# The first norms of a two-branch transformer block become steps of the expert units' schedule

## The reference, cut to what matters

```python
xn = layernorm(x)                      # the first norm: (x - mean) / sqrt(var + eps)
out = x + encoder(xn) + experts(xn)

def experts(x):                        # one attention of 8 heads, no mask
    xn = layernorm(x, norm_w, norm_b)
    q, k, v = project(xn)              # token quarter e reads only the first 128 / 2**e features
    a = softmax(q @ k.T * 128 ** -0.5) @ v
    return out_project(a) + x          # again cut to 128 / 2**e features

def encoder(x):                        # 4 layers, 16 heads, causal with ALiBi
    for i in range(4):
        x = x + mha(layernorm(x, ln1_w[i], ln1_b[i]))
        x = x + ffn(layernorm(x, ln2_w[i], ln2_b[i]))      # gelu, 512 hidden
    return layernorm(x, final_w, final_b)
```

## Time and profile before

| | |
|---|---|
| median of three runs | 1554.06 us |
| the profiled execution, its own time | 1555.07 us |
| its span, first to last instruction | 1553.0 us |
| TensorE busy | 1424.0 us (92%) |
| ScalarE busy | 1232.2 us (79%) |
| VectorE busy | 1069.0 us (69%) |
| GpSimd busy | 633.2 us (41%) |
| mean granted TensorE clock | 0.973 |

### The profile page before, as it was taken

One profiled execution on the slowest core, in us unless ns is written; L12 is line 12 of the kernel. 1 busy time (PEld: TensorE's weight loads), 2 busy tenths in 40 slices (PEclk: granted clock), 3 DMA queues, 4 the chain that ended last, 5 costly groups with the idle time before them and its releaser, 6 DMA issues.

```text
span 1553.0 us, 39617 instructions
## 1 busy us (share of the span) xinstructions
PE 1424.0 (92%) x10720; PEld 934.6 (60%) x10720; DVE 1069.0 (69%) x2802; ACT 1232.2 (79%) x2181; POOL 633.2 (41%) x1087
## 2 busy tenths in 40 slices
PE   2779997599999999999999999999999999999995
PEld 2455554256666666666666666666666666666653
DVE  5677774366777777777777767777777777777762
ACT  3334454178899999999999989999999999999884
POOL 4444444333333333333333333333333345555443
PEclk9989997689999999999999999999999999999998
DMA  6324441244444454544444445444444455444430
GB/s 181 103 83 123 122 122 62 82 122 115 128 123 128 123 127 124 143 134 128 123 122 123 129 128 136 129 128 130 122 123 131 135 142 135 133 130 129 127 93 11
DMA packets 106534, 187.78 MB, mean 121 GB/s; under 512 B 20104, under 2 KB 72456, under 8 KB 106448
## 3 DMA queue, kind: packets, MB, share of 16 engines
q1 hardware_dynamic: 91632, 150.45, 34.9%
q0 software_dynamic: 14848, 36.72, 9.0%
HBM read 120.87 MB, written 65.01 MB: 120 GB/s over the span
## 4 chain that ended last, share of the span: by engine, by line
PE 65%; DVE 13%; issue 9%; DMA 5%; ACT 3%; POOL 3%; SPq 1%; DVEq 0%; POOLq 0%; ACTq 0%
PE pvp L1141 13%; DVE negm L815 10%; PE mxp L1084 10%; PE exp_ps L1118 9%; PE dense L1182 6%; PE mxp L1030 6%; PE mxp L1088 6%; PE dense L1059 4%; PE dense L1170 3%; DMA blocks<-split_L 3%; PE mxp L1069 2%; PE dense L1030 2%; PE mxp L1159 2%; PE mxp L1059 1%; DMA split_F<-lo 1%
## 5 line engine op out<-in xcount | busy, mean ns | idle before, releaser
L815 DVE TENSOR_REDUCE negm<-mxp 128x2 f32<-128x512 f32 x896 | 568.1, 685 | 58.1 <-PE mxp L1088 55.1
L974 ACT ACTIVATE probs<-exp_ps 128x512 f32<-128x512 f32 x896 | 514.5, 593 | 105.9 <-PE exp_ps L1118 99.0
L1118 PE MATMUL exp_ps<-qbd_l,kst_l 128*128 128x512 f32 x768 | 346.6, 479 | 14.1 <-ACT exp_ps L1003 10.5
L1084 PE MATMUL mxp<-blocks,qst 104*128 104x512 f32 x768 | 333.6, 466 | 6.1 <-DMA blocks<-split_L 5.5
L1003 ACT ACTIVATE exp_ps<-masktf 128x512 f32<-128x512 f32 x513 | 308.7, 602 | 22.1 <-POOL rest L671 5.8
L1088 PE MATMUL mxp<-maskb,identb 128*128 128x256 bf16 (+1 forms) x768 | 247.6, 322 | 0.0
L613 POOL TENSOR_TENSOR lo<-y,hi 128x512 fp32r<-128x512 f32 x80 | 102.6, 1282 | 268.2 <-DVE hi L790 268.2
L1141 PE MATMUL pvp<-probs,vst_l 128*32 128x256 f32 (+1 forms) x4096 | 207.3, 332 | 0.0
L1084 PEld LDWEIGHTS mxp<-blocks,qst 104*128 104x128 f32 x768 | 148.2, 193 | 48.2 <-issue 31.0
L1141 PEld LDWEIGHTS pvp<-probs,vst_l 128*32 128x32 f32 x4096 | 111.0, 109 | 95.1 <-issue 36.6
L1088 PEld LDWEIGHTS mxp<-maskb,identb 128*128 128x128 bf16 x768 | 75.1, 98 | 148.9 <-issue 133.3
(11 more groups left out here) (99 smaller groups left out, 1922.6 us busy)
## 6 DMA issues: line engine op xcount, KB each, us to landing
split_L<-hi SPq DMA_DIRECT2D x256, 128.0 KB, 2.1
qst<-split_L SPq DMA_DIRECT2D x64, 384.0 KB
kst_l<-split_L SPq DMA_DIRECT2D x64, 384.0 KB
qbd_l<-split_L SPq DMA_DIRECT2D x256, 96.0 KB
split_L<-lo POOLq DMA_DIRECT2D x128, 128.0 KB, 2.3
blocks<-split_L POOLq DMA_DIRECT2D x128, 96.0 KB, 4.2
blocks<-split_L SPq DMA_DIRECT2D x128, 96.0 KB
split_F<-hi SPq DMA_DIRECT2D x64, 128.0 KB, 2.1
```

Source lines behind the costliest of these rows:

```text
L815: dve.tensor_reduce(heads[:, g, first:first + count], bank[MAX_BANK + k % 3].rearrange("p (h t) -> p h t", h=count), AX.X, ALU.max, negate ...
L974: act.activation(probs[:, g, ch, :], exp_ps[:, k % 2, :], ACT.Exp, scale=plan.scale).then_inc(q.b_exp, 1)
L1084: pe.matmul(o, qst[0:BIAS_END, g, qt * P:(qt + 1) * P], kbd[0:BIAS_END, first:first + count, g, 0:keys], start=True, stop=True, skip_group ...
L1118: last = pe.matmul(o, kst[plan.name][:, s, g, kt * P:(kt + 1) * P], rhs, start=seeder not in ("ACT", "DVE"), stop=True, skip_group_check=True)
```

## The change

What it does, piece by piece:
- The norms of quarters 1 to 3 are no longer made in blocks. "first" is a step of the experts' slots, directly in front of "ln", for the units from 4 on: VectorE normalises one sequence.
- The statistics of quarters 2 and 3, and VectorE's wait for the remaining weights, stand behind the slot that prepares unit 0. The deviations of these quarters are made on GpSimd between the early and the late steps of the next slot, which is split in two for all engines.
- The four clears of `qbd_l` move from GpSimd to ScalarE, behind its first rounding; they are written as a copy of the identity with scale 0.
- The clear of `blocks` stands in front of the last round of the experts' slots (`scored`), behind a wait for all exponent matmuls.
- VectorE no longer waits for all expert sums in front of the encoder's rounds, and ScalarE waits for the last products with the values instead.

```diff
--- before.py
+++ after.py
@@ -106,7 +106,7 @@
                 + part("f1", s - 1, 1) + part("pv", s, 2) + at("smaxp", s + 2) + end_sum + at("xn", s + 3)
                 + end2 + part("pv", s, 3) + at("w:w1", s) + at("v", s + 2) + store)
         return (
-                part("pv", s - 1, 2) + at("ln", s + 2) + at("stack> v", s + 1) + part("pv", s - 1, 3)
+                part("pv", s - 1, 2) + at("first ln", s + 2) + at("stack> v", s + 1) + part("pv", s - 1, 3)
                 + at("pv+", s - 1) + at("rstd xt", s + 2) + at("ot", s - 1) + at("row>", s) + at("xn", s + 2)
                 + at("op", s - 2) + at("xb", s - 1) + at("v+", s + 1) + at("negt+", s) + at("xt+", s + 2)
                 + at("ot+", s - 1) + at("y qk", s + 2) + at("op+", s - 2) + at("hi", s + 2) + part("max", s + 1, 0)
@@ -125,6 +125,8 @@
         for step, off, *k in sum((list(self.slot_steps(s, last_layer)) for s in slots), []):
             u = 2 * n + off
             if early is not None and early != (step in EARLY or step[0] == "w"):
+                continue
+            if step == "first" and isinstance(n, int) and u < QUARTER:
                 continue
             if not isinstance(n, int) or 0 <= u < self.units:
                 yield step, u, off % 2, n + off // 2, k[0] if k else 0, off
@@ -227,12 +229,17 @@
         eng.wait_ge(q.lo_parts[s], 16 * 2 * EXPERT.rounds)
 
 
-def expert_rounds(eng, experts, encoder, join, between=(None, None, None, None)):
-
-    for k, (n, slots) in enumerate(((-1, (0,)), (-1, (1,)), (0, (0, 1)), (1, (0, 1)))):
-        experts(n, slots=slots)
-        if between[k] is not None:
-            between[k]()
+def expert_rounds(eng, experts, encoder, join, first_done=None, projected=None, scored=None):
+
+    experts(-1, slots=(0,))
+    if first_done is not None:
+        first_done()
+    experts(-1, slots=(1,), early=True)
+    if projected is not None:
+        projected()
+    experts(-1, slots=(1,), early=False)
+    experts(0)
+    experts(1)
     with eng.Fori(2, EXPERT.rounds - 1) as n:
         experts(n)
     experts(EXPERT.rounds - 1, slots=(0,))
@@ -240,6 +247,8 @@
     encoder(-2, early=True)
     encoder(-1, slots=(0,), early=True)
     experts(EXPERT.rounds - 1, slots=(1,))
+    if scored is not None:
+        scored()
     experts(EXPERT.rounds)
 
 
@@ -696,27 +705,19 @@
             def encoder(n, **part_of_round):
                 steps(ENCODER, n, **part_of_round)
 
-            def clear_queries(k):
-                pool.memset(qbd["L"][0:ALIBI_ROW, k // 2, 8 * (k % 2):8 * (k % 2) + 8, :].bitcast(F32), 0.0).then_inc(s_initv, 1)
-
             def second_half_of_deviations():
                 for k in range(2, 4):
                     inverse_deviation_of_quarter(k, k + 1)
-                clear_queries(0)
-
-            def clear_more_queries():
-                clear_queries(1)
-                clear_queries(2)
+
+            def clear_blocks():
+                pool.wait_ge(S["F"].b_s, EXPERT.exp_chunks * GROUPS * EXPERT.units)
+                pool.memset(blocks[0:ALIBI_ROW].bitcast(F32), 0.0).then_inc(s_cleared, 1)
 
             def join():
-                clear_queries(3)
                 pool.wait_ge(s_w, 16 * 3)
                 wait_for_projections(pool, S["F"])
 
-            expert_rounds(pool, experts, encoder, join,
-                          (None, None, second_half_of_deviations, clear_more_queries))
-            pool.wait_ge(S["F"].b_s, EXPERT.exp_chunks * GROUPS * EXPERT.units)
-            pool.memset(blocks[0:ALIBI_ROW].bitcast(F32), 0.0).then_inc(s_cleared, 1)
+            expert_rounds(pool, experts, encoder, join, projected=second_half_of_deviations, scored=clear_blocks)
             pool.wait_ge(s_cleared, 1)
             pool.sem_inc(s_final, 2)
             for s in range(2):
@@ -740,15 +741,16 @@
                     last = dve.bn_aggr(mv_all[:, r, :], stats_all[:, r, :])
                 last.then_inc(s_mv, 1)
 
-            def first_norm(k):
-
-                dve.wait_ge(s_rstd, k + 1)
-                for b in range(k * QUARTER, (k + 1) * QUARTER):
-                    for t in range(NT):
-                        r = b * NT + t
-                        last = dve.tensor_scalar(state[:, b, t, :], rest[:, b, t, :], mv_all[:, r, 0:1],
-                                                 rstd_all[:, r:r + 1], ALU.subtract, ALU.mult)
-                    last.then_inc(s_norm, 1)
+            rstd_each = rstd_all.rearrange("p (r k) -> p r k", k=1)
+
+            def first_norm(b, quarter):
+
+                dve.wait_ge(s_rstd, quarter + 1)
+                for t in range(NT):
+                    r = b * NT + t
+                    last = dve.tensor_scalar(state[:, b, t, :], rest[:, b, t, :], mv_all[:, r, 0:1],
+                                             rstd_each[:, r, :], ALU.subtract, ALU.mult)
+                last.then_inc(s_norm, 1)
 
             def quarter_statistics(k):
                 dve.wait_ge(s_x[k], 16)
@@ -757,7 +759,8 @@
 
             quarter_statistics(0)
             quarter_statistics(1)
-            first_norm(0)
+            for b in range(QUARTER):
+                first_norm(b, 0)
             dve.wait_ge(s_w_first, 16 * 2)
 
             def statistics(q, stage, u, s, source):
@@ -831,7 +834,9 @@
                 q = S[plan.name]
                 for step, u, s, r, k, _ in plan.steps(n, last_layer, **part_of_round):
                     bt = u % BATCH if plan.causal else u
-                    if step == "ln":
+                    if step == "first":
+                        first_norm(u, 3 if not isinstance(u, int) or u >= 2 * QUARTER else u // QUARTER)
+                    elif step == "ln":
                         if plan.causal:
                             dve.wait_ge(q.c_done, u + 1)
                         else:
@@ -923,14 +928,9 @@
             def second_half_of_statistics():
                 quarter_statistics(2)
                 quarter_statistics(3)
-
-            def second_half_of_norms():
-                first_norm(2)
-                first_norm(3)
-
-            expert_rounds(dve, experts, encoder, join,
-                          (lambda: first_norm(1), lambda: dve.wait_ge(s_w, 16 * 3), second_half_of_statistics, second_half_of_norms))
-            dve.wait_ge(S["F"].c_done, BATCH)
+                dve.wait_ge(s_w, 16 * 3)
+
+            expert_rounds(dve, experts, encoder, join, first_done=second_half_of_statistics)
             encoder_rounds(dve, encoder)
 
         @block.scalar
@@ -944,6 +944,11 @@
 
             act.wait_ge(s_rows_first, 16)
             round_rows(0)
+            act.wait_ge(s_init, 5)
+            for k in range(4):
+                nothing = ident[0:ALIBI_ROW, :].unsqueeze(1).to_broadcast([ALIBI_ROW, ENCODER.heads, P])
+                part = qbd["L"][0:ALIBI_ROW, k // 2, 8 * (k % 2):8 * (k % 2) + 8, :].rearrange("p h (a t) -> p (h a) t", t=P)
+                act.activation(part, nothing, ACT.Copy, scale=0.0).then_inc(s_initv, 1)
             act.wait_ge(s_w_first, 16 * 2)
 
             def steps(plan, n, last_layer=False, **part_of_round):
@@ -1015,8 +1020,8 @@
                 round_rows(2)
 
             expert_rounds(act, experts, encoder, lambda: wait_for_projections(act, S["F"]),
-                          (round_other_rows, None, None, None))
-            act.wait_ge(S["F"].c_done, BATCH)
+                          first_done=round_other_rows)
+            act.wait_ge(S["F"].b_pv, GROUPS * EXPERT.units)
             for k in range(2):
                 if SEEDER.get(k) == "ACT":
                     seed(k)
@@ -1212,7 +1217,7 @@
                 pe.wait_ge(s_w, 16 * 3)
 
             expert_rounds(pe, experts, encoder, lambda: wait_for_projections(pe, S["F"]),
-                          (None, others_loaded, None, None))
+                          projected=others_loaded)
             pe.wait_ge(s_ones, 1)
             pe.wait_ge(s_bias, 16 * ENCODER.hg)
             encoder_rounds(pe, encoder)
```

## The result

The changed kernel takes **1541.67 us** (median of 4 executions, 1537.37 to 1543.29) beside 1553.9 (1552.52 to 1554.81, 4) for the kernel before: ratio 0.9918, 95% interval 0.9896 to 0.9939, faster by 0.8%. Forecast were 1546.5 and a range of 1537.0 to 1552.5. The profiled execution took 1543.29 with a span of 1541.5; 1547.5 had been worked out for it. I set the experiments against that.

A forecast was written before the change was run, and what follows sets the result against it. The expert part was taken as a ring of latencies, ahead of encoder layers mostly on TensorE. Terms -15.8 + 9.0 + 6.1 - 6.9 = -7.6 took 1555.07 to 1547.5 us, hence median 1546.5; range 1537 to 1552.5.

The forecast's parts named there:

- u0 to u2: From unit 0's to unit 2's inverse deviation on GpSimd: forecast 9.0 us longer.
- SP's reordering: SP's queue: unit 0's stacks load behind unit 1's high-part stores, shifting the ring by +9.0 us, bounds +7 to +11.
- statistics: Statistics and deviations of quarters 2 and 3, moved behind unit 0: cost 0, bounds 0 to 1 for VectorE's work.
- u2 to u15: From unit 2's to unit 15's inverse deviation: forecast -9.7 us, stalls and steps together.
- stalls: Expert ring: without the two insertions, four long periods fall to 13.24 us each, saving 15.8.
- steps: First norms directly ahead of "ln" in units 4 to 15: 0.51 us per period, +6.1, bounds 0 to +11.
- u15 to m: From unit 15's inverse deviation to the encoder's first maxima: forecast 6.9 us shorter.
- clear of `blocks`: Join to the encoder: the earlier clear brings the encoder's first maxima forward, -6.9 us, bounds -4 to -10.
- SP's order is not free: Answers the rival that SP's reordering at unit 0's maxima costs nothing: -16.6, 1537.5 us, chance 0.12.
- the steps are not hidden where they stand: Answers the rival that the norm steps ahead of "ln" are hidden: -13.7, 1540.4 us, chance 0.11.
- the encoder's opening gains: Answers the rival that the encoder's opening does not gain: -0.7, 1553.4 us, no change, chance 0.10.
- that rival: TensorE's granted clock falls in all twelve periods, each paying 1.0 us: +4.6 in all, 1558.7, slower, chance 0.07.

The follow-up runs named there:

- e1: Changed kernel, but SP runs slot 1 of round -1 in one piece, loading unit 0's stacks before storing unit 1's high part: 1536.23 us.
- e13: Changed kernel with statistics and deviations of quarters 2 and 3 back behind round 0, the clears staying on ScalarE: 1548.97 us.
- e7: e5 plus GpSimd's deviations of quarters 2 and 3 split over units 1 and 2, and its first encoder stacks right behind the clear of `blocks`: 1528.06 us.
- e5: Changed kernel with the edits of e1 and e3 together, nothing else: 1531.28 us.
- e4: Kernel before with only the first norms of quarters 1 to 3 made as steps; statistics and GpSimd's clears stay between the rounds: 1553.45 us.
- e3: Changed kernel with each norm step made one unit earlier, behind "ln" instead of in front of it: 1538.72 us.
- e2: Changed kernel with `blocks` cleared behind the expert rounds again, not in front of the last out-projections: 1550.36 us.
- e6: Changed kernel with VectorE's and ScalarE's waits for all expert sums restored: 1539.71 us; e6_again, unchanged on another chip: 1541.19 us.
- e10: Changed kernel with the four clears of `qbd_l` on GpSimd, behind its two deviation steps, not on ScalarE: 1541.58 us.

## Why the prediction was right

The direction, the mechanism of each large term and the range held; the size was 4.8 short. By the traces, before to after:

| term | predicted | trace |
|---|---|---|
| u0 to u2 (SP's reordering, statistics) | +9.0 | +8.1 |
| u2 to u15 (stalls -15.8, steps +6.1) | -9.7 | -11.1 |
| u15 to m (clear of `blocks`) | -6.9 | -9.0 |
| rest | 0 | +0.4 |
| sum | -7.6 | -11.6 |

*SP's reordering.* `kst_f` was forecast at 36.9 and went out at 37.16, the landing at 41.7 and TensorE started at 42.05: 4.47 behind the issue of `blocks`, beside 4.4 before. So the estimate of 1.0 for sharing the DMA engines with the low-part copies was not paid by SP's stack. It showed on the other side: those two copies landed after 3.5 at the median, 2.3 before, and GpSimd waited 0.63 for them ahead of unit 1's stack. The sixteen matmuls took 4.77, 0.30 each, not 6.1, the 0.38 each read from a shorter run; that 1.3, less the 0.35 by which they started later than 41.7, is the 0.9. e1 shows that 6.5 of the 8.1 are SP's order.

*Statistics behind unit 0.* "0" was right for VectorE (e13: behind round 0, statistics and deviations together cost 6.8), and in this kernel it was right for GpSimd as well, because SP's stacks were later still. But the deviations that stand in front of unit 1's stack cost up to 1.7 once SP is on time (e1), 1.3 of it shown for one of the two quarters (e7 against e5). The prediction put them at 0 (its bounds of 0 to 1 stand at the work of VectorE), reasoning that no maximum reads that stack before unit 2 has been projected; it left out that GpSimd issues the stack ahead of unit 2's own inverse deviation.

*Stalls and steps.* From unit 3 to 15 the periods gave 174.66 - 163.38 = 11.3, forecast 9.7. A step costs 0.38 by the period of the whole stretch, 0.42 by the eight behind unit 7 ((225.76 - 116.47) / 8 = 13.66), 0.50 in e4, and was forecast at 0.51; the slack of 0.22, an average of nine units, was read too small: 0.73 of work that costs 0.38 leaves 0.35, and in unit 15 GpSimd idles 0.39. e3 confirms the cause: behind "ln" the step is free.

*The clear.* The term that was mis-sized most. After the stacks' issue it went as forecast (3.05 to the maxima, 3.15 worked out). But the issue itself moved by 5.4 against unit 15's start, and 3.5 were taken. The rest: GpSimd's sequencer waits 0.32 for its issue, not 1.09 (0.7 to 0.8), and the last sums come 1.1 earlier behind unit 15, 0.8 of it ahead of the first product. e2 gives the edit alone as 7.35 in the trace. The other 1.65 is mostly the length of the last products of probabilities and values, 3.66 before and 2.67 in e2: from the last exponent matmul to the end of the last sum it is 10.88 before and 9.54 in e2. That length follows TensorE's granted clock. Before, then after (windows over these 32 matmuls, read as the earlier trace rows):

```profile
271.54:275.20 3.66, 3.65 (x33) 1.45 (x32) 0.10 (x1) 0.60 (x1) 0.00 (x0) 0.50 0.01 2
268.28:271.40 3.12, 3.11 (x33) 1.37 (x32) 0.10 (x1) 0.60 (x1) 2.99 (x1) 0.61 0.01 3
```

At 0.50, the lower of the two levels (1.2 of 2.4 GHz), throughout, they take 3.66; at a mean of 0.61 it is 3.12, at 0.72 (e2) 2.67, at 0.81 (e6) 2.40. The change doesn't decide it: e3, with the join of the kernel after, has 0.51 and 3.66 again. So the 1.1 by which the last sums come earlier is luck of the two traces: 0.5 lies in these products, 0.3 in the out-projection behind them (1.04 at 278.38 before, 0.71 at 274.59 after), 0.3 ahead of the last exponent matmul. The fourth clear of `qbd_l`, gone from the join too, isn't it: e4 still has it there, and its way from the last exponent matmul to the last sum is 9.75, its products 2.84.

*ScalarE's clears and the dropped waits*: 0 and 0. The clears took 7.31 for 7.4 and stayed hidden. The waits change nothing up to the encoder's first maxima (e6, e6_again); behind them it is open.

*The rivals.* SP's order is not free (e1), the steps are not hidden where they stand (e3), and the encoder's opening gains (e2). The clock does drop in one of the twelve periods (0.88 from 130.22 to 144.27), but its 14.05 is the longest of them, and the mean is 13.61, not the 13.24 + 1.5 that rival needed.

## What to carry to other kernels

When a program's order is cut into an early and a late half for the sake of two engines, ask for each other queue what its late half now stands behind; here leaving one engine's list whole was worth 6.0 us, on top of a gain of 12.2. A small operation in a ring of latencies is free directly behind the handover that its engine next waits on, and in front of it costs its length less the slack there: 0.38 of 0.73. Work that was hidden behind a stall comes out when the stall is mended, so edits to one stall have to be made, and measured, together.

## What the runs showed of the hardware

VectorE's scalar operation on fp32 tiles stood still while GpSimd cleared memory. VectorE's L749 in the kernel before, all its sixteen operations of the second stall (count, then min/median/max in ns, first and last start), then the two long ones among them, with GpSimd's timeline at the same time:

```profile
L749 DVE TENSOR_SCALAR state<-rest,mv_all,rstd_all x16: 328/340/4061, 99.8 to 107.2; 128x128 f32<-128x128 f32 x16
L749 DVE TENSOR_SCALAR state<-rest,mv_all,rstd_all x2: 3871/3966/4061, 100.6 to 100.8; 128x128 f32<-128x128 f32 x2
```

```profile
100.99 3.57 POOL L700 MEMSET qbd_l<- 96x2048 f32 x2
```

The median is 340 ns; two, started at 100.58 and 100.84, take 4061 and 3871 and end at 104.6 to 104.7, just behind the clears, which run from 100.99 to 104.56. Elsewhere in the row one starts every 0.26; here the next starts 3.8 later. So 3.5 of that stall were the clears, and the sixteen norms alone some 4.2 (e4, which took them away, shortened the period by 4.0). The same shows in small in most units. VectorE's `xn` beside GpSimd's `xb`, kernel before:

```profile
54.78 0.71 POOL L662 TENSOR_TENSOR xb<-state,rest 128x256 f32<-128x256 f32 x1
54.83 1.01 DVE L783 TENSOR_SCALAR xn<-state,mv,rstd 128x128 f32<-128x128 f32 x2 [1.47 <-POOL rstd L579]
```

The two take 1.01 there and 0.60 in unit 0, where nothing of GpSimd's runs beside them. The reductions from PSUM don't mind: eight take 4.88 beside e10's clears and 4.88 without. This agrees with the Trainium skill, "SBUF — State Buffer", section "Who interferes with whom": an operation in VectorE's two-port mode and a GpSimd operation exclude each other, whoever is first, for a whole instruction. Which of VectorE's modes these operations ran in no trace shows.

The second thing is the spread named above: executions of one kernel differ by 1 to 11 us (e1: 1535.66 to 1536.69; e4: 1547.25 to 1558.7). Between traces most of it sits in the landing of the input's second quarter, up to 2.6, and in the encoder's 1255 to 1262; 0.2 to 1.5 sits in each column of the edited part.
